# A decoder layer on one core: fewer Newton rounds, norms and verdict beside the context projections, merged masks, two banks for the first self sums

## The reference

```
x = x + attn(layernorm(x))            # causal self attention, 16 heads of 8, scores / sqrt(128)
x = x + xattn(layernorm(x), ctx)      # cross attention on 6404 context rows of 96, heads of 8
x = x + ffn(layernorm(x))             # 8 experts of 128 -> 512 -> 128, the two best per row, gated

def _layernorm(x, axis=-1, eps=1e-05):
    m = jnp.mean(x, axis=axis, keepdims=True)
    v = jnp.var(x, axis=axis, keepdims=True)
    return (x - m) / jnp.sqrt(v + eps)
```

## Time and profile before

| | us |
|---|---|
| median of 3 runs | 1010.72 |
| the three runs | 1008.5, 1010.72, 1015.35 |
| profiled execution, its own time | 1012.52 |
| span of its trace | 1010.6 |
| TensorE busy / ScalarE busy in the span | 878.2 / 868.4 |

### The profile page before, as it was taken

One profiled execution on the slowest core, in us unless ns is written; L12 is line 12 of the kernel. 1 busy time (PEld: TensorE's weight loads), 2 busy tenths in 40 slices (PEclk: granted clock), 3 DMA queues, 4 the chain that ended last, 5 costly groups with the idle time before them and its releaser, 6 DMA issues.

```text
span 1010.6 us, 14927 instructions
## 1 busy us (share of the span) xinstructions
PE 878.2 (87%) x6128; PEld 257.8 (26%) x6128; DVE 178.0 (18%) x537; ACT 868.4 (86%) x664; POOL 8.6 (1%) x33
## 2 busy tenths in 40 slices
PE   6978888999888888888899888888888888899997
PEld 4552222222111111111112211111111111134443
DVE  6755644320000000000003000000000000043212
ACT  4656888999999999999999999999999999943332
POOL 3000000000000000000000000000000000000000
PEclk9985999999999999999999999999998999999999
DMA  4251006511112111111221111111221000020200
GB/s 142 105 188 38 1 2 117 182 32 32 35 38 51 43 34 32 32 35 34 42 55 33 36 32 35 35 32 41 41 46 35 3 1 1 1 85 1 84 11 10
DMA packets 19717, 46.32 MB, mean 46 GB/s; under 512 B 6210, under 2 KB 9388, under 8 KB 19132
## 3 DMA queue, kind: packets, MB, share of 16 engines
q1 hardware_dynamic: 19644, 45.31, 17.9%
HBM read 38.18 MB, written 7.11 MB: 45 GB/s over the span
## 4 chain that ended last, share of the span: by engine, by line
PE 34%; issue 31%; ACT 31%; DVE 3%; DMA 0%; ACTq 0%; DVEq 0%
ACT probs L696 31%; PE psum L1341 10%; PE psum L1311 6%; PE psum L1561 5%; PE psum L1573 5%; PE psum L1210 1%; PE psum L1244 1%; PE psum L1458 1%; DVE turned L914 1%; PE psum L1248 1%; PE psum L1337 1%; PE psum L1231 0%; PE psum L1444 0%; PE psum L1194 0%; DVE xn L787 0%
## 5 line engine op out<-in xcount | busy, mean ns | idle before, releaser
L696 ACT ACTIVATE probs<-psum 128x1536 f32<-128x1536 f32 (+1 forms) x520 | 784.3, 1777 | 36.9 <-PE psum L1311 24.6
L1341 PE MATMUL psum<-probs,v_ctx 128*9 128x512 f32 x3200 | 422.6, 600 | 3.1 <-DVE turned L914 2.7
L1311 PE MATMUL psum<-q_all,k_ring 32*128 32x512 f32 (+1 forms) x1792 | 266.1, 496 | 106.1 <-ACT probs L696 100.4
L1311 PEld LDWEIGHTS psum<-q_all,k_ring 32*128 32x128 f32 x1792 | 103.7, 186 | 503.1 <-ACT probs L696 452.1
L914 DVE STREAM_TRANSPOSE turned<-psum 128x512 f32<-128x512 f32 x16 | 11.5, 717 | 626.2 <-PE psum L1337 609.0
L748 ACT ACTIVATE probs<-psum,b_sb 128x512 f32<-128x512 f32 x64 | 44.0, 687 | 71.9 <-PE psum L1561 71.8
L1341 PEld LDWEIGHTS psum<-probs,v_ctx 128*9 128x9 f32 x3200 | 47.6, 88 | 104.7 <-issue 97.7
L1561 PE MATMUL psum<-xnT,w_region 128*128 128x512 f32 x128 | 65.3, 594 | 1.9 <-issue 1.9
L1573 PE MATMUL psum<-probs,ctx_region 128*128 128x512 f32 x128 | 65.0, 592 | 0.0
L1341 PE MATMUL psum<-probs,v_self 128*9 128x512 f32 (+3 forms) x384 | 43.3, 553 | 2.9 <-DVE turned L914 1.7
L1573 PEld LDWEIGHTS psum<-probs,ctx_region 128*128 128x128 f32 x128 | 24.3, 190 | 30.6 <-issue 30.6
(11 more groups left out here) (144 smaller groups left out, 251.3 us busy)
## 6 DMA issues: line engine op xcount, KB each, us to landing
k_ring<-kc_parts SPq DMA_DIRECT2D x256, 52.0 KB
k_ring<-kc_parts SPq DMA_DIRECT2D x256, 48.0 KB
kc_parts<-kparts_bc SPq DMA_DIRECT2D x8, 512.0 KB, 2.8
probs<-gate_rows SPq DMA_DIRECT2D x4, 1024.0 KB, 6.0
kc_parts<-probs SPq DMA_DIRECT2D x4, 512.0 KB, 2.8
w_region<-in_L_ffn_W SPq DMA_DIRECT2D x1, 2048.0 KB, 13.3
ctx_region<-in_ctx SPq DMA_DIRECT2D x1, 768.0 KB, 7.8
ctx_region<-in_ctx SPq DMA_DIRECT2D x1, 672.0 KB, 6.3
```

What stands on the lines that cost most here:

```text
L696: act.activation(probs[:, slot:slot + w, :], psum[:, at:at + w, :], ACT.Exp, scale=SC[ph]).then_inc(L[ph]["exp_done"], 1)
L1311: mm = pe.matmul(into[:, col:col + n_q], keys, q_all[rows, g, hf * HALF + q0:hf * HALF + q0 + n_q], start=True, stop=True)
L1341: mm = pe.matmul(into[:, q0:q0 + w], v_all[:, h, t, :], probs[:, place(ph, at)[1], col:col + w], start=first, stop=last)
```

## The change

Six things are done. The rows of both halves are normalised together at the start, and every normalisation has three Newton rounds instead of four. TensorE loads the verdict on the self attention between the chunks 6 and 7 of the context and only branches at the gate. The norms of the keys are formed beside the projections: 24 after chunk 7, four after each later chunk, 11 at the end. VectorE makes `ctailT` one chunk earlier. At the gate TensorE no longer waits for `outs_cleared`; its first sum does. The masks of neighbouring banks are multiplied in one instruction. In the first half of the self attention the sums of quads 1 and 3 go to bank 6.

```
+def sum_bank(ph, half, g):
+    return OUT_BANK - (ph == 0 and half == 0) * (g % 2)
...
 def diagonals(group):
-    return [(place(0, at)[1], col) for at in range(first, first + w) ...]
+    blocks = sorted((col, place(0, at)[1]) for at in range(first, first + w) ...)
+    runs = []
+    for col, at in blocks:
+        if runs and runs[-1][2] == col and sum(runs[-1][:2]) == at:
+            runs[-1][1] += 1
+        else:
+            runs.append([at, 1, col])
+    return runs
...
+        def verdict_of(eng, ph):
+            eng.wait_ge(s["bounded_made"], ph + 1)
+            return eng.value_load(bounded[0:1, ph:ph + 1], min_val=0, max_val=1)
...
-                for _ in range(4):
+                for _ in range(3):
                     step(dve.scalar_tensor_tensor(newton[:, here], rstd[:, here], -0.5, rstd[:, here], ALU.mult, ALU.mult))
...
             for hf in range(NHALF):
                 dve.wait_ge(s[f"x_loaded{hf}"], 16)
                 stats_of(hf)
-                normalise_rows(hf)
+            normalise_rows(0, NHALF)
...
-                if c == NCHUNK - 1:
+                if c == NCHUNK - 2:
                     dve.wait_ge(s["ones_made"], 2)
                     dve.wait_ge(s["ctxT_done"], NCHUNK)
...
-                    dve.transpose(turned[:, hf, :], bank(OUT_BANK)).then_inc(L[ph][f"turned{hf}"], 1)
+                    dve.transpose(turned[:, hf, :], bank(sum_bank(ph, hf, g))).then_inc(L[ph][f"turned{hf}"], 1)
...
-                            for at, col in diagonals(group):
-                                here = probs[:, at, col:col + P]
-                                ins = dve.tensor_tensor(here, here, causal[:, :], ALU.mult)
+                            for at, n_at, col in diagonals(group):
+                                here = probs[:, at:at + n_at, col:col + P]
+                                ins = dve.tensor_tensor(here, here, causal[:, :].unsqueeze(1).to_broadcast([P, n_at, P]),
+                                                        ALU.mult)
...
+                if c == 6:
+                    self_bounded = verdict_of(pe, 0)
+                if c == 7:
+                    norms_of_ctx(range((c - 1) * CHUNK), c - 1)
+                elif c > 7:
+                    norms_of_ctx(range((c - 2) * CHUNK, (c - 1) * CHUNK), c - 1)
+            norms_of_ctx(range((NCHUNK - 2) * CHUNK, KT + 1), NCHUNK).then_inc(s["norms_ctx"], 1)
...
-                        if n:
+                        if ph == 0 and g < 2 and hf == 0:
+                            pass
+                        elif ph == 0 and (hf == 0 or g == 0):
+                            pe.wait_ge(L[0]["turned0"], (QUADS if hf else g) - 1)
+                        elif n:
                             pe.wait_ge(L[ph][f"turned{batches[n - 1][1]}"], turned_of[batches[n - 1][1]])
-                        elif ph == 1:
+                        if ph == 0 and n == 0:
+                            pe.wait_ge(s["outs_cleared"], 1)
+                        elif ph == 1 and n == 0:
                             pe.wait_ge(s["attnT_done"], 2)
...
-            pe.wait_ge(s["outs_cleared"], 1)
...
-            choose(pe, 0, self_attention, general_self)
+            pe.cond(self_bounded, self_attention, general_self)
```

38 lines of the change are left out of this document (19 added, 19 removed).

## The result

| | before | after |
|---|---|---|
| median of 5 runs, us | 1010.72 (1008.5 to 1015.35) | 1004.54 (1002.45 to 1005.74) |
| profiled execution, us (span) | 1012.52 (1010.6) | 1005.74 (1003.8) |
| first exponential, us | 71.79 | 68.73 |
| fifteenth exponential, us | 102.03 | 95.99 |
| length at granted clock 0.50, first 100 us | 13.6 + 13.6 | 10.2 + 6.8 |

The changed kernel was timed again later, on another occasion, beside the kernel before: 1003.27 against 1011.75, 0.9929 [0.9903, 0.9955]. The forecast was 1006.4: a gain of 4.35 us, where 6.2 and 8.5 were measured. From the fifteenth exponential on the two traces run nearly side by side: it is 6.0 us earlier, and the end of the span 6.8. So nearly all of the explanation lies in the first 96 us.

The account below looks back on a forecast made before the run. The prediction took TensorE as the bound in the context and the last store as the bound at the gate. Its terms summed to −4.35 us from a median of 1010.72, giving 1006.4, with an 8-in-10 range of 1000 to 1013.

Parts of the forecast that it names:

- start: Normalising both halves' rows together lets the projection of the first queries begin at 15.1 instead of 16.07 us: −1.0.
- norms in mid-stream: In the context, 40 norms stand ahead of the last chunk's keys on a TensorE without pauses: +1.1, up to +1.4.
- load of the verdict: Between context chunks 6 and 7, the load takes TensorE's stream some time while queued transposes run: +0.2, ends 0 and +0.7.
- `ctailT`: Made earlier, it no longer stands in front of the context's last subtraction and the store behind it: −0.1.
- gate: First exponential of the self attention at 68.65 instead of 71.79, bounded by the last store and not by TensorE: −3.15.
- two banks: In the self attention's first half, three waits of TensorE's sums on the transposition go: −1.1, ends −0.6 and −1.5.
- masks: In the self attention's first half, merged mask instructions shorten TensorE's one visible wait on masks: −0.3, ends 0 and −1.0.
- Newton rounds elsewhere: Rounds saved beside the attentions and the experts' products lie behind other work: 0, end −0.6.
- the prediction's own sign of being wrong: The prediction is wrong if low-clock stretches in the first 100 us differ from two; its other such signs concern load and scores.
- The clock stays up: Rival: TensorE's shorter pause at the gate keeps 2.4 GHz: 1002.4 us, or 1000.1 without the second low stretch; chance 0.15.
- The clock comes back late: Slower rival: the self attention's low stretch goes on, each further 13.6 us costing 3.6; two give 1013.5 us; chance 0.13.
- the change gives little: Rival: costly norms and load, and ScalarE's branch fetching code at the gate, leave only the low end, 1009.3 us; chance 0.14.

Follow-up runs that it names:

- e1: The kernel before with only the gate's part: TensorE loads the verdict in mid-stream and its first sum waits for the clear; 1007.53 us, ratio 0.995.
- e6: The changed kernel with all 51 norms behind the last product of the context, as before the change; 1003.74 us, ratio 0.9886.
- e3: The changed kernel with bank 7 alone for every quad's sums; 1005.96 us, ratio 0.9951.
- e4: The changed kernel with one mask instruction for each block; 1005.78 us, ratio 0.9938.
- e7: e6, with ScalarE waiting for the key stores only ahead of its third group's exponentials and VectorE loading its verdict in mid-context; 1001.74 us, ratio 0.9891.
- e10: The changed kernel itself, timed again on another occasion beside the kernel before; 1003.27 us, ratio 0.9929.
- e8: The changed kernel with full-array products that nobody reads filling TensorE's pauses at the gate and in the first groups; 1002.05 us, ratio 0.988.
- e11: e8, with VectorE's units of quads 0 to 2 placed behind the masks of the next group; 999.59 us, ratio 0.9878.
- e12: e9 with e11's order: norms last, stores waited for later, filling, and units behind the next masks; 996.28 us, ratio 0.9843.
- e9: e7 with filling products in TensorE's pauses, fewer of them at the gate than in e8; 998.93 us, ratio 0.9894.
- e5: The changed kernel with the two halves normalised one after the other, with three Newton rounds each; 1004.46 us, ratio 0.9917.

## Why the prediction was right, and where its size was off

**The parts.** The sum was −4.35; the runs at equal low clock give −4.7 ± 0.4. Term by term:

| term | forecast | measured | by |
|---|---|---|---|
| start | −1.0 | −1.06, mean of eleven profiles (−2.5 to +0.2) | quad products, 21.29 before and in e1 |
| norms in mid-stream | +1.1 | +1.18 | e6 against the change |
| load of the verdict | +0.2 | +0.01 | e1 |
| `ctailT` | −0.1 | −0.11 | quad to first, e6 against e1 |
| gate | −3.15 | −3.19 | e1 |
| two banks | −1.1 | −0.8 ± 0.5 at equal low clock; −1.26 in one profile, clock included | e3 |
| masks | −0.3 | −1.0 ± 0.6 | e4 |

The start depends on the execution, since TensorE, no longer VectorE, now sets when it ends; with a spread of 2.7 us the close agreement of its mean with the forecast is partly luck. `ctailT` took a wait of 0.95 us from TensorE, but no more than the forecast's 0.1 from the path. From quad to first the four terms between the start and the first exponential sum to −1.95, and 50.50 became 48.38: −2.12. The claim on which most hung, that the store and not TensorE would set the first exponential, is shown by the chain after, by e1, and by e7, in which removing that wait moved the exponential 1.7 us beyond e6. The Newton rounds elsewhere can't be told from nothing: beyond the fifteenth exponential the kernel gained 0.8 us in all.

**The clock.** This term was mis-sized. The sum has none for the clock, which the prediction took as neutral between two rivals; among its signs is a granted clock of 0.50 twice in the first 100 us. It was twice in one profile of the change and once in the other, where the prediction's own sign of being wrong is met, and shorter in both: over all runs the mean at the low clock fell from 42.1 to 29.5 us (standard errors 1.0 and 2.2), which at 0.31 is −3.9 us. With −4.7 that makes −8.6, which is the difference of the mean spans (1010.7 to 1002.1, 42 and 11 executions) by the way the line is drawn. In the two profiled executions 10.2 us less in the first 100 are worth 3.2. So something like 3 to 4 us of the gain came from what the forecast had at zero, and the median of 1004.54 lies 1.9 us below the 1006.4 for it.

The price itself the prediction had nearly right: its 7 × (1.94 − 1.43) = 3.6 us per 13.6 is 0.26 per microsecond, against 0.31. *The clock stays up* had the mechanism half right. The shorter pause didn't keep the clock: it fell at 68.8, with 1.19 us of work in the 4.20 before it, as the prediction had argued against that rival. In e10 it fell as well, but the second fall was gone, and seven exponentials took 10.51 where the rival gave 12.0. Full-array work in the pauses did keep the clock: of 14 profiled executions the three with no low stretch in the first 100 us are e8, e11 and e12, and e9 has 3.4 us. No run filled the pauses with narrow products, so that the products must fill the array isn't shown. The times that the rival gave, 12.0 for the eighth exponential and 12.0 more for the next seven, came out in e8 as 12.43 and 10.51. The Trainium skill (TensorE: Matmul & The Clock Gate, Why this matters for your kernels) warns of one long gap between bursts; here the clock also fell at 154.1, after a stretch in which TensorE was busy 2.12 of 4.10 us in short pieces with no pause over 1.14, so the long gap isn't the whole account. *The clock comes back late* didn't happen on average in the change, but single executions show it: e5 and e4 had stretches of 17 us.

```profile
68.00:85.20 17.20, 12.71 (x82) 4.32 (x82) 7.79 (x19) 10.10 (x8) 0.00 (x0) 0.51 0.42 101
```

This window of e5 has TensorE busy for 12.71 of 17.20 us at 1.2 GHz. In the kernel before, the time at the low clock runs from 26 to 53 us between executions, worth 8 us by the slope, more than any single part of the change.

**Two slips in its numbers.** The rival *the change gives little* names three causes, but with these alone the sum is −1.0 + 1.4 + 0.7 − 0.1 − 2.4 − 1.1 − 0.3 = −2.8, or 1007.9; its 1009.3 needs every term at its low end. And a difference under 1% isn't one that can't be told from none: the measured 0.8% has an interval that leaves out 1.

**What stays open.** Why the clock returns sooner in the changed kernel than in the one before. The kernels with only a part of the change (e1 to e5) have means between 32.8 and 37.1 us, with standard errors of 2 to 4.5, so what each part brings can't be told; and e6, without the norms in mid-stream, has the same 29.5 as the change; no run separates the pauses' length from the kind of products between them.

## What to carry to other kernels

When several engines meet at a gate, list for each one what it waits for there; taking away the latest wait is worth the distance to the next latest and no more, and work that is hidden behind the one that remains (here the norms, beside a store that takes 2.58 us to land) must not be moved to where its engine is full. Before costing an edit, see whether the runs of one kernel scatter with the granted clock: here the runs of one kernel lay up to 12.6 us apart, with 0.31 us for each microsecond at the low clock, and an edit's parts can be read only at equal low clock. If TensorE is about to enter a stretch of narrow products after a pause, full-array products that nobody reads can pay for themselves: e8 added such work to TensorE's pauses and its mean span was 999.9 us against 1002.1 (the difference ± 1.1), and e12, which has some too, is clearly faster.

## What the runs showed of the hardware

- A register load from SBUF in the middle of TensorE's stream lasted 0.78 us in e1 and cost 0.01 us there. In the kernel after it lasted 0.79, from 48.7 to 49.5, and TensorE was busy without a pause from 48 to 61: products that stood ahead of the load ran meanwhile.
- TensorE at 1.2 GHz did not get its full clock back in 13.6 us in which it was busy 11.77 with products of 32 rows and of 9-column weights. The same kinds of products ran in the stretch from 82.4 of the kernel after, which ended after 6.8 us with 5.19 busy. The low stretch at 154.1 ended after 3.4 us, and began with two products that fill the array, 2.07 us long; narrow ones followed. No run separates the kind of products from the rest.

```profile
154.28 2.07 PE L1486 MATMUL psum<-xnT,w_quads 128*128 128x512 f32 x2
```

- In the first 16 us the granted clock is recorded as 1.00, yet transposes of 128 columns take 0.25 us each in one execution (three in 0.74 before) and 0.13 in another (e3, eight in 1.04). When TensorE gets past this differs between executions with the same start, whose quad products begin from 18.84 to 21.50: a scatter that the granted clock doesn't show.

```profile
12.17 1.04 PE L1201 MATMUL psum<-ident,xn 128*128 128x128 f32 x8
```

That is e3's timeline, with the eight transposes of `xn`, to hold against 1.58 us for the same eight in the kernel after.
